# The attention mask goes into the banks of scores by a ScalarE copy instead of a TensorE product, with a new order of work

## What is computed

```
x = x + layernorm(attention(layernorm(x)))             # parts before the layers
h = layernorm(x)
for i in range(6):                                     # "the layers"
    q, k, v = split(shift(h) @ Wqkv[i])                # 16 heads of 64
    q, k = l2norm(q) * qs, l2norm(k) * ks, then rotary with a scale
    # windows of 32 queries, each sees its own 32 keys and the 32 before
    sim = 8 * q k^T;  sim = where(mask, -big, sim)
    h = softmax(sim) @ v @ Wo[i] + h
    n = norm(shift(h)) * g + b
    h = (a * gelu(gate)) @ W2[i] + b2 + h              # a, gate = n @ W1[i] + b1
x = x + layernorm(h)
```

## Time and profile before

| | |
|---|---|
| median of 3 runs | 4550.41 us (4549.1 to 4551.08) |
| the profiled execution | 4545.86 us, span 4544.1 us |
| mean granted clock of TensorE | 0.967 |
| busy share of the span | PE 93%, PEld 65%, DVE 81%, ACT 79%, POOL 51% |
| the layers | from about 1031 us to 4497 us |

### The profile page before, as it was taken

How to read it: one execution, slowest core, us unless ns; L and a number is a source line. 1 busy time by engine, 2 the same in 40 slices (tenths; PEclk the granted TensorE clock), 3 DMA queues, 4 the chain that set the end, 5 groups by cost and what they waited for, 6 DMA issues and landing times. The chain is left out here.

```text
span 4544.1 us, 138566 instructions
## 1 busy us (share of the span) xinstructions
PE 4209.9 (93%) x44000; PEld 2967.1 (65%) x44000; DVE 3701.0 (81%) x8420; ACT 3584.1 (79%) x6842; POOL 2338.2 (51%) x2840
## 2 busy tenths in 40 slices
PE   4899999966999999999999999999999999999994
PEld 2466666644766767767776677767777766776673
DVE  6688888876888888888888888888888888888884
ACT  1799999935888888888888888888888888888883
POOL 1000000016666666666666666666666666666671
PEclk7899999978999999999999999999999999999997
DMA  6677777712111111111111111111111111111111
GB/s 221 216 231 231 231 231 231 231 55 73 33 44 42 41 45 32 41 45 41 45 32 41 45 41 42 35 41 46 41 39 38 41 46 41 36 41 41 45 41 48
DMA packets 258908, 361.00 MB, mean 79 GB/s; under 512 B 44404, under 2 KB 216156, under 8 KB 257884
## 3 DMA queue, kind: packets, MB, share of 16 engines
q1 hardware_dynamic: 258140, 351.55, 25.7%
HBM read 151.19 MB, written 93.34 MB: 54 GB/s over the span
## 5 line engine op out<-in xcount | busy, mean ns | idle before, releaser
L1367 PE MATMUL la_ps<-la_Wqkv,la_xsT 128*128 (+1 forms) x2304 | 1201.1, 617 | 8.5 <-DVE la_rsk L1081 5.3
L1024 POOL TENSOR_TENSOR la_rt<-la_rt,la_rn 128x1024 f32<-128x1024 f32 x384 | 722.4, 1902 | 27.5
L1081 DVE TENSOR_TENSOR la_rsq<-la_ps,la_tab 128x1024 f32<-128x1024 f32 x384 | 469.7, 1223 | 140.9 <-ACT la_sq L1225 138.3
L1225 ACT ACTIVATE la_sq<-la_ps 128x512 f32<-128x512 f32 x768 | 453.7, 596 | 152.3 <-issue 62.0
L1088 DVE TENSOR_REDUCE la_ssum<-la_sq 128x8 f32<-128x512 f32 x768 | 502.6, 674 | 51.4 <-issue 51.4
L1402 PEld LDWEIGHTS la_ps<-la_kT,la_qB 128*64 128x64 f32 x12288 | 391.8, 138 | 146.7 <-issue 145.8
L1367 PEld LDWEIGHTS la_ps<-la_Wqkv,la_xsT 128*128 128x128 f32 x2304 | 378.6, 191 | 158.5 <-issue 121.3
L1081 DVE TENSOR_TENSOR la_rsk<-la_ps,la_tab 128x1024 f32<-128x1024 f32 x384 | 465.8, 1213 | 4.1 <-ACT la_sq L1225 3.9
L1433 PEld LDWEIGHTS la_ps<-la_Wo,la_oT 128*128 128x128 f32 x3072 | 365.1, 192 | 133.2 <-issue 132.3
L1402 PE MATMUL la_ps<-la_kT,la_qB 128*64 128x64 f32 x12288 | 435.1, 224 | 0.0
L122 POOL TENSOR_TENSOR la_ln_stats<-la_ln_stats,la_ln_power 128x1 f32<-128x1 f32 x192 | 105.4, 549 | 615.0 <-DVE la_ln_stats L117 615.0
(11 more groups left out here) (168 smaller groups left out, 10272.1 us busy)
## 6 DMA issues: line engine op xcount, KB each, us to landing
at_band<-skew_scratch SPq DMA_DIRECT2D x64, 1536.0 KB, 7.3
la_vs<-la_v SPq DMA_DIRECT2D x192, 384.0 KB, 3.5
skew_scratch<-at_R SPq DMA_DIRECT2D x64, 1024.0 KB, 6.7
la_vs<-la_v SPq DMA_DIRECT2D x192, 128.0 KB, 3.4
la_Wqkv<-in_wqkv SPq DMA_DIRECT2D x28, 384.0 KB, 3.6
kt_scratch<-pr_k SPq DMA_DIRECT2D x24, 384.0 KB, 3.2
qt_scratch<-pr_q SPq DMA_DIRECT2D x24, 384.0 KB, 4.0
at_qh<-qt_scratch SPq DMA_DIRECT2D x64, 144.0 KB
```

The costliest lines, as they stand in the source:

```text
L1024: e.tensor_tensor(heads(rt, w), heads(rt, w), wide(rn[:, w * H:(w + 1) * H], D), ALU.mult)\
L1081: e.tensor_tensor(dst.rearrange("p f (h d) -> p f h d", d=D), ps[:, c % 2, :].rearrange("p (h d) -> p h d", d=D).unsqueeze(1).to_broadcast ...
L1225: e.activation(sq[:, c % 2, :], ps[:, c % 2, :], ACT.Square).then_inc(sq_ev.sem, 1)
L1367: e.matmul(ps[:, c % 2, :], xsT[:, m * P:(m + 1) * P], Wqkv[:, ds(layer(n) % 2, 1), c * 512:(c + 1) * 512], start=True, stop=True)\
```

## The change

The mask is kept in f32 alone. PE's `masked` goes. In its place ACT copies the f32 mask (128 columns, repeated four times) into the bank of scores; `scores` waits for that copy. Before the first turn PE writes each of the two banks once with `start=True`, after which the products of `scores`, all with `start=False`, add to what stands in the bank. The bf16 mask and identity, with one load and two casts, go. The order of the steps is laid out anew on all five engines. The diff, without its declarations:

```diff
@@ -916,7 +916,6 @@
                 mark.open(e)
             for dst, src in ((lng, "lngT"), (lnb, "lnbT"), (b1, "b1T"), (mask32, "c_mask"), (rot, "c_rot")):
                 e.dma_start(dst[:], a[src]).then_inc(s_in, 16)
-            e.dma_start(sq[:, 0, 0:P], a["c_ident"]).then_inc(s_in, 16)
             e.dma_start(scales[:], a["scales"].partition_broadcast(P)).then_inc(s_in, 16)
             e.dma_start(b2[:], a["L0_ffn_b2"].partition_broadcast(P)).then_inc(s_in, 16)
 
@@ -959,14 +958,13 @@
                 e.dma_start(Y[0:1, m + 1, D:2 * D], Y[P - 1:P, m, 2 * D:3 * D]).then_inc(ys_in[m % 2].sem, 16)
 
             def body(t):
+                for n, m in t.back(7):
+                    next_layer(n, m)
+                for n, m in t.back(2):
+                    y_shifted(n, m)
+                    w1_in(n, m)
                 for n, m in t.back(0):
                     v_shifted(n, m)
-                for n, m in t.back(1):
-                    y_shifted(n, m)
-                for n, m in t.back(2):
-                    w1_in(n, m)
-                for n, m in t.back(3):
-                    next_layer(n, m)
             rounds(e, body, TILES, TB, DEEPEST)
             for mark in (w_qkv, w_o, w_2):
                 e.wait_ge(mark.sem, mark.v(DEPTH))
@@ -1043,22 +1041,23 @@
                                 ALU.add).then_inc(yb_ev.sem, 1)
 
             def body(t):
-                for n, m in t.back(7):
-                    root(n, m)
                 for n, m in t.back(4):
                     added(n, m, 0)
                     added(n, m, 1)
                     newton(n, m)
                     scaled(n, m, 0)
-                    scaled(n, m, 1)
-                for n, m in t.back(2):
-                    table(n, m)
-                for n, m in t.back(6):
-                    with_b2(n, m)
                 for n, m in t.back(0):
                     x_copied(n, m)
                 for n, m in t.back(4):
+                    scaled(n, m, 1)
+                for n, m in t.back(7):
+                    with_b2(n, m)
+                for n, m in t.back(1):
+                    table(n, m)
+                for n, m in t.back(4):
                     carried(n, m)
+                for n, m in t.back(6):
+                    root(n, m)
             rounds(e, body, TILES, TB, DEEPEST)
 
         @block.vector
@@ -1067,9 +1066,6 @@
                 mark.open(e)
             e.memset(xsT[D:P, 0:1], 0.0).then_inc(s_set, 1)
             e.wait_ge(s_in, 16 * N_IN)
-            e.tensor_copy(mask[:], mask32[:])
-            e.tensor_copy(identb[:], sq[:, 0, 0:P]).then_inc(s_mask, 1)
-            e.wait_ge(s_mask, 1)
             e.wait_ge(s_set, 2)
 
             def turned(n, m, c):
@@ -1153,8 +1149,10 @@
                                 yb[:, (m - 1) % 4:(m - 1) % 4 + 2, :], ALU.add).then_inc(x_ev.sem, 1)
 
             def body(t):
-                for n, m in t.back(3):
-                    squares(n, m, 1)
+                for n, m in t.back(5):
+                    summed(n, m, 1)
+                for n, m in t.back(3):
+                    turned(n, m, 2)
                 for n, m in t.back(5):
                     over_sum(n, m, 1)
                 for n, m in t.back(6):
@@ -1165,47 +1163,44 @@
                     turned(n, m, 3)
                     squares(n, m, 2)
                     squares(n, m, 3)
+                    clipped(n, m)
+                for n, m in t.back(4):
+                    largest(n, m, 0)
+                    below(n, m, 0)
+                    largest(n, m, 1)
+                    below(n, m, 1)
                 for n, m in t.back(7):
                     if m % 2:
                         next_x(n, m)
-                for n, m in t.back(3):
-                    clipped(n, m)
-                for n, m in t.back(4):
-                    largest(n, m, 0)
-                    largest(n, m, 1)
-                    below(n, m, 0)
-                    below(n, m, 1)
+                for n, m in t.back(4):
                     summed(n, m, 0)
                 for n, m in t.back(6):
                     if m % 2:
                         gated(n, m, 0)
                 for n, m in t.back(2):
                     turned(n, m, 0)
-                    squares(n, m, 0)
-                for n, m in t.back(4):
-                    over_sum(n, m, 0)
                 for n, m in t.back(5):
                     with_x(n, m)
                 for n, m in t.back(4):
+                    over_sum(n, m, 0)
                     normal(n, m, 0)
                 for n, m in t.back(6):
                     if m % 2:
                         gated(n, m, 1)
                 for n, m in t.back(2):
+                    squares(n, m, 0)
                     turned(n, m, 1)
-                    turned(n, m, 2)
-                for n, m in t.back(5):
-                    stats(n, m)
+                    squares(n, m, 1)
                 for n, m in t.back(6):
                     if m % 2:
                         gated(n, m, 2)
-                for n, m in t.back(4):
-                    summed(n, m, 1)
+                for n, m in t.back(5):
+                    stats(n, m)
             rounds(e, body, TILES, TB, DEEPEST)
 
         @block.scalar
         def _(e):
-            for mark in (xT_ev, sq_ev, v_ev, r_ev, c_ln, Tq_ev, Tk_ev, ex_ev, pt_ev, o_ev, yn_ev, nT_ev, g_ev):
+            for mark in (mk_ev, xT_ev, sq_ev, v_ev, r_ev, c_ln, Tq_ev, Tk_ev, ex_ev, pt_ev, o_ev, yn_ev, nT_ev, g_ev):
                 mark.open(e)
             e.wait_ge(s_in, 16 * N_IN)
             e.wait_ge(s_set, 2)
@@ -1257,6 +1252,12 @@
                 e.activation(kT[:, 4 * u:4 * u + 4, at:at + P], ps[:, BANK_T, :].rearrange("p (j t) -> p j t", j=4),
                              ACT.Copy).then_inc(Tk_ev.sem, 1)
 
+            def masked(n, m, h):
+
+                e.wait_ge(nm_ev.sem, nm_ev.v(n - 1, h + 1))
+                e.activation(ps[:, BANK_S + h, :].rearrange("p (j c) -> p j c", j=4), over(mask32[:, min(m, 1), :], 4),
+                             ACT.Copy).then_inc(mk_ev.sem, 1)
+
             def exp(n, m, h):
                 e.wait_ge(sub_ev.sem, sub_ev.v(n, h + 1))
                 e.activation(ps[:, BANK_S + h, :], ps[:, BANK_S + h, :], ACT.Exp).then_inc(ex_ev.sem, 1)
@@ -1294,38 +1295,24 @@
 
             def body(t):
                 for n, m in t.back(3):
-                    squared(n, m, 1)
-                    squared(n, m, 2)
-                for n, m in t.back(4):
-                    k_turned(n, m, 0)
-                for n, m in t.back(5):
-                    p_turned(n, m, 0)
-                for n, m in t.back(7):
-                    if m % 2:
-                        gelu(n, m, 2)
-                        e.preload_act_table_set(LN_AND_EXP)
-                for n, m in t.back(5):
-                    exp(n, m, 1)
-                for n, m in t.back(4):
-                    q_turned(n, m, 1)
+                    squared(n, m, 3)
                 for n, m in t.back(0):
                     x_turned(n, m)
-                for n, m in t.back(3):
-                    squared(n, m, 3)
+                for n, m in t.back(5):
+                    o_out(n, m, 0)
                 for n, m in t.back(6):
                     one(n, m)
-                for n, m in t.back(5):
-                    o_out(n, m, 0)
-                for n, m in t.back(3):
-                    v_out(n, m, 4)
                 for n, m in t.back(4):
                     k_turned(n, m, 1)
+                    masked(n, m, 1)
                 for n, m in t.back(5):
                     p_turned(n, m, 1)
                 for n, m in t.back(3):
                     guess(n, m)
                 for n, m in t.back(6):
                     y_turned(n, m)
+                for n, m in t.back(3):
+                    v_out(n, m, 4)
                 for n, m in t.back(5):
                     o_out(n, m, 1)
                 for n, m in t.back(4):
@@ -1341,6 +1328,22 @@
                 for n, m in t.back(6):
                     if m % 2:
                         gelu(n, m, 1)
+                for n, m in t.back(2):
+                    squared(n, m, 1)
+                for n, m in t.back(3):
+                    masked(n, m, 0)
+                    k_turned(n, m, 0)
+                for n, m in t.back(2):
+                    squared(n, m, 2)
+                for n, m in t.back(6):
+                    if m % 2:
+                        gelu(n, m, 2)
+                        e.preload_act_table_set(LN_AND_EXP)
+                for n, m in t.back(4):
+                    exp(n, m, 1)
+                    p_turned(n, m, 0)
+                for n, m in t.back(3):
+                    q_turned(n, m, 1)
             rounds(e, body, TILES, TB, DEEPEST)
 
         @block.tensor
@@ -1349,7 +1352,10 @@
                 mark.open(e)
             e.wait_ge(s_in, 16 * N_IN)
             e.wait_ge(s_set, 2)
-            e.wait_ge(s_mask, 1)
+
```

(53 more changed lines are left out.)

## The result

The changed kernel takes 4567.15 us (median of 6 runs, 4563.31 to 4569.13), the kernel before in the same rounds 4549.74 (4548.23 to 4551.08): ratio 1.0038, 95% interval 1.0026 to 1.005. It is 17 us slower, where 74 us faster was forecast. One execution among all the runs, of e5_cut_pe, took 5960 us at a mean clock of 0.646; it is left out of every number here. The profiled execution has a span of 4565.5 us and a mean clock of 0.954 (before: 4544.1 and 0.967).

What follows compares the result with a forecast made beforehand. PE was taken as the fullest engine, 33.1 of a pair's 34.3 us. 96 pairs by -0.8 gave -77, the start +3, together -74 us: 4476 us, with a range of 4430 to 4565.

Steps and rivals of the forecast that it cites:

- Step 7: Loop's branch, now behind back_out on PE: PE's own stall sets the loss as before, nothing counted, 1 us either way.
- no term: PE's clock: gaps under a microsecond each, clock 1.00 in pairs with such gaps, so nothing was added for it.
- A larger loss at the branch: Listed sign that would make the forecast wrong, at the loop's branch; no size given.
- Step 1: Masks off PE: 384 bf16 products go, 0.84 us a pair, PE's need falling from 33.1 to 32.3.
- Steps 3 to 5: New waits and order placed over two turns: odd 18.3, even 14.9, pair 33.2; with an allowance, 33.5 us.
- step 5: Allowance for the late second scaled before turn_k 0 and for DVE's clipped before guess: 0.3 us, bounds 0 and 1.0.
- Steps 2 and 8: ACT mask copies: 0.585 to 0.615 us, step 0.49, 1.96 a pair; start of layers: 3 us later.
- Step 6: SP's loads and shifts reordered, next_layer later: costs nothing; without its cover, under 15 us in all.
- ACT takes the gain back: Rival: fuller ACT and late evictions give PE 0.5 to 0.8 us more gaps a pair, 4524 to 4553; chance 0.15.
- Slower: ACT's waits don't shrink enough: Rival: at the odd turn's end ACT's waits give only 1.5 us or nothing, 4597 to 4740; chance 0.18.

Runs made afterwards that it cites:

- e5_cut_pe: The changed kernel with only TensorE's loop cut moved back to where the kernel before has it: 4544.6 us, ratio 0.9995.
- e1: The changed kernel, same sequence, with the loop cuts of TensorE, ACT, DVE and POOL moved back to where the kernel before has them: 4519.7 us.
- e4: The changed kernel with the mask left out on every engine, a measure only since it computes something else: ordinary pair 33.95 us.
- e2: The changed kernel, its order and cuts kept, with the masks again bf16 products on TensorE and no ACT copies: ratio 1.003.
- e7: The changed kernel with the masks again bf16 products on TensorE and all loop cuts moved back: 4488.8 us, ratio 0.9871.
- e12: The changed kernel with the loop cuts of ACT, DVE and POOL moved back and TensorE's left in its new place: 4644.7 us.
- e8: The changed kernel with all cuts moved back and ACT's eviction v_out 4 put ahead of guess and y_turned: 35 us slower than e1.

## Why the prediction was wrong

Per pass of the loop it had 4 pairs by -0.8; measured are 3 by -0.28 and one by +1.89. So the loop is 4.25 us worse than forecast, 89 us over 21 passes of the 95 by which the two spans differ. About half of that is the branch itself, 2.17 us more than before over an ordinary pair and 46 in all; the other half is that the ordinary pair, which the forecast took for all four of a pass, misses by 0.52, 44 us in all.

- **Step 7, the branch, and "no term" for the clock: half of the miss.** The step was "PE's own stall sets the loss as before, so I count nothing", with 1 us either way. Measured: the pair at a branch is 6.75 us longer than an ordinary one, where it was 4.58. The stall did not stay as it was: by the same measure TensorE stands 2.76 us in the mean for 2.33 before, and stands again in scores. What comes behind it changed too, and with it the clock: 0.92 over the pair at all 22 branches, where before has 1.00 at half of them and 0.96 at the others. I had the mean of 0.92 over one turn in the earlier trace rows before me and read it as a property of the branch; it was a thing that the place of the cut could make worse. Moving the cuts back gave 52 us; e1's own branches show 2.1 us between clock held and clock lost. "A larger loss at the branch" stood among the signs of being wrong, but with no price. The Trainium skill (TensorE: Matmul & The Clock Gate, Part 1, What's actually happening) says that half clock is the default and activity releases it. The trace agrees: after 2.99 us without a product the first two windows show 0.50 and the third 0.88.
- **Step 1, masks off PE as a gain of 0.84 a pair: wrong.** It rests on "PE is the fullest engine", which is right, and on reading that as PE setting every turn. e4 against e2 gives +0.11 for the whole removal, or -0.07 in the two pairs without the wait ahead of stats. My own placing had half of the answer: it put the even turn at 14.9 with 14.1 of work for PE, so that turn had gaps of 0.8 and did not end on TensorE's work, and its 0.42 of masks could give nothing. Measured, from e2 to e4, the even turn grew by 0.18, and the odd one gave 0.25 of its 0.42 in the same two pairs.
- **Steps 3 to 5, the placing: too short by 0.5 a pair.** The even turn came to 15.4 to 15.6 for 14.9, the odd one to 18.4 to 19.1 for 18.3; step 5's allowance of 0.3 was to cover this and did not. Of the miss, 0.7 in one pair of three is the wait ahead of stats, which I had not placed at all because the DMA of y is on SP's queue. That the new sequence is worth something is right: e7 has 33.73 for 34.43.
- **Steps 2 and 8: right.** Copy, step, ACT's sum and the 3 us at the start are as forecast. Step 6, SP: no wait of TensorE for a weight showed up.
- **The rivals.** "ACT takes the gain back" comes nearest in kind: in the ordinary pair the mask as copies costs 0.31 to 0.40 us more than as products, 0.20 of it by the comparison with e4, which has neither. "Slower: ACT's waits don't shrink enough" had the right sign and the wrong mechanism: ACT's waits did shrink (88.5 to 5.5), and values and turn_k 1 did wait, but at the branch, for TensorE at half clock. That the sequence alone, at the old cuts, is worth 59 us, and the mask minus 24, no rival had.

What stays open: why TensorE's clock falls at some branches and not at others of the same kernel, why TensorE stands a second time in scores, 0.6 us of the cuts' 2.05, and why the old sequence with copies loses another 1.8 at the branch (40.82) with the clock low in only 2 of 22.

## What to carry to other kernels

Where a loop is cut is a decision of its own: the same sequence ran at 4520, 4567 or 4645 us by the places of the branches alone, so after any relayout compare the stretch at the branch first, see whether the stands of engines that feed each other overlap or add up, and look at the granted clock behind them. An engine that is fullest by its busy share doesn't pass on what is taken from it unless the turn in question ends on it: ask in which turn the work lies, and what the next wait in that turn is. The version to keep is the new sequence with the masks left on TensorE and the old cuts: 4488.8 us, ratio 0.9871 [0.9855, 0.9887].

## What the runs showed of the hardware

- At a loop's branch an engine can stand for 2 to 3 us: in the rows above TensorE 2.99 and DVE 3.30 in the changed kernel, ACT 2.32 and DVE 2.41 in e12; in the changed kernel ACT stood only 0.63. The Trainium skill (Advanced Engine Details and Errata, Control Flow Timing) gives about 51 ns for a branch and 108 for a compare-and-branch; the stands of TensorE and DVE are some 20 to 30 times the larger figure, and the measurement decides. That they are all the branch instruction's own is not shown.
- The same branch in the same execution kept TensorE's clock at 1.00 or lost it (12 and 7 of 22 in e1), at 2.1 us. Some kernels with such branches scatter from run to run (e5 by 28 us, e8 by 16, against 6 us of the changed kernel, which loses it always), but e7, with 6 such branches, by 3 only.
- A copy of 128x512 from SBUF to PSUM on ACT costs the step of one from PSUM (0.48 to 0.52 us), and TensorE added the scores onto what ACT had put into the bank, all 384 times.
